# The maxima of the next chunk two slots later, and the expert weights at the end of a step

## The reference, cut to what matters

```
xn = _layernorm(x)
attention: Q, K, V = low-rank projections of layernorm(xn) + bias
  scores = where(causal, Q K^T / sqrt(8), -1e9);  ctx = softmax(scores) V
  h = xn + ctx @ out_U @ out_V + out_b
  branch 1 = h + gelu(layernorm(h) @ fc1_U @ fc1_V + fc1_b) @ fc2_U @ fc2_V + fc2_b
experts: top 2 of softmax(xn @ Wr), weights cw normalised over the two
  branch 2 = sum over e of cw[e] * ((silu(xn @ Wg[e]) * (xn @ Wu[e])) @ Wd[e])
out = x + branch 1 + branch 2
```

## Time and profile before

| | |
|---|---|
| time, median of 3 runs | 1030.21 us (1029.5 to 1030.91) |
| time of the profiled execution | 1029.5 us |
| its span | 1027.8 us |
| TensorE matmul | 965.2 us (94%) |
| TensorE weight load | 751.1 us (73%) |
| VectorE | 701.6 us (68%) |
| ScalarE | 539.0 us (52%) |
| GpSimd | 431.2 us (42%) |
| steps 0 to 15 of the attention | about 100.5 to 617 us |

### The profile page before, as it was taken

The page is one execution under the profiler, slowest core; times in us unless marked ns, Lnnn a source line. Parts: engine busy times, 40 slices in busy tenths (PEclk is TensorE's granted clock), DMA queues, the critical chain, the costliest instruction groups (busy, mean ns, idle before and its releaser), DMA issues. The chain is left out here.

```text
span 1027.8 us, 25266 instructions
## 1 busy us (share of the span) xinstructions
PE 965.2 (94%) x7701; PEld 751.1 (73%) x7701; DVE 701.6 (68%) x3192; ACT 539.0 (52%) x1256; POOL 431.2 (42%) x563
## 2 busy tenths in 40 slices
PE   4767999999999999999999988999999999999997
PEld 3535566666666666666666647999999999999986
DVE  5557688877778778777777853565565554558887
ACT  1552355555555555555555664555555555554442
POOL 9361132154544544435555422554544544540100
PEclk9585899999999999999999998999999999999999
DMA  8284454354554555353443204222222222238784
GB/s 234 72 236 136 168 178 174 106 154 135 130 142 130 141 143 136 99 135 111 140 116 117 80 28 123 64 64 66 68 69 63 66 64 62 74 111 248 208 224 134
DMA packets 133558, 127.13 MB, mean 124 GB/s; under 512 B 17274, under 2 KB 113652, under 8 KB 133428
## 3 DMA queue, kind: packets, MB, share of 16 engines
q1 hardware_dynamic: 109860, 67.83, 24.3%
q0 software_dynamic: 20592, 56.43, 17.8%
q10 hardware_dynamic: 2976, 1.26, 0.5%
HBM read 57.15 MB, written 42.60 MB: 97 GB/s over the span
## 5 line engine op out<-in xcount | busy, mean ns | idle before, releaser
L1393 DVE CUSTOM_DVE_ANT_0 att_masked_st<-att_m_ps,att_mask_st 128x128 bf16<-128x128 f32 (+1 forms) x1024 | 311.0, 353 | 106.9 <-PE att_m_ps L999 61.0
L817 ACT ACTIVATE att_probs<-att_t_ps 128x512 f32<-128x512 f32 x384 | 229.2, 598 | 211.1 <-PE att_t_ps L1023 204.6
L1641 POOL DMA_INDIRECT y_scratch<-moe_y,moe_row_now x136 | 132.2, 972 | 152.6 <-DVE moe_y L1895 109.3
L652 POOL DMA_INDIRECT slot_x<-att_xs,att_slot_now x128 | 126.8, 991 | 164.2 <-PE att_t_ps L1023 145.7
L1889 DVE TENSOR_TENSOR moe_hidden<-moe_gate,moe_up_ps 128x352 f32<-128x352 f32 x136 | 70.9, 521 | 112.8 <-ACT moe_gate L1816 111.6
L1023 PE MATMUL att_t_ps<-att_mask_ts,att_ident_b 128*128 128x256 bf16 (+1 forms) x384 | 123.7, 322 | 0.0
L1718 PE MATMUL moe_y_ps<-w_down,moe_hidden_t 128*128 (+1 forms) x816 | 113.9, 275 | 1.4 <-DVE moe_y L1895 1.2
L1816 ACT ACTIVATE moe_gate<-moe_gate_ps 128x352 f32<-128x352 f32 x136 | 63.0, 463 | 96.5 <-PE moe_up_ps L1701 96.5
L1718 PEld LDWEIGHTS moe_y_ps<-w_down,moe_hidden_t 128*128 128x128 f32 (+1 forms) x816 | 101.8, 191 | 2.7 <-issue 2.6
L1393 DVE DVE_READ_ACCUMULATOR2_ANT att_row_max<- 128x1 f32 x1024 | 84.6, 83 | 0.1
L1022 PE MATMUL att_t_ps<-att_odd_stack,att_k_stack 97*128 97x512 f32 x192 | 81.3, 424 | 3.0 <-DMA att_odd_stack<-att_neg_max 2.6
(11 more groups left out here) (264 smaller groups left out, 2067.3 us busy)
## 6 DMA issues: line engine op xcount, KB each, us to landing
att_k_stack<-att_qk_parts POOLq DMA_DIRECT2D x96, 128.0 KB, 3.4
slot_x<-att_xs POOLq DMA_DIRECT2D x17, 516.0 KB, 3.2
moe_x<-slot_x SPq DMA_DIRECT2D x34, 258.0 KB, 2.8
att_xs<-xn_scratch SPq DMA_DIRECT2D x32, 256.0 KB
mlp_rows<-y_scratch POOLq DMA_DIRECT2D x16, 512.0 KB, 5.3
even_stack<-att_qk_parts SPq DMA_DIRECT2D x192, 32.0 KB
att_odd_stack<-att_qk_parts SPq DMA_DIRECT2D x192, 32.0 KB
xn_scratch<-att_probs POOLq DMA_DIRECT2D x16, 256.0 KB, 3.0
```

What stands on the lines that cost most here:

```text
L652: pool.indirect_dma_start(env["slot_x"][:], bass.IndirectOffsetOnAxis(ap=slot_now[c.parity][:, col:col + 1], axis=0), xs[c.parity][:, t, k ...
L817: act.activation(probs[:, m % PT, :], t_ps[m % 2][:], ACT.Exp).then_inc(exp_done, 1)
L1393: last = dve.tensor_tensor_reduce(out=masked_st[m % 2][:, part], in0=m_ps[m % 2][:, part], in1=mask_st[:, SEQ - width:], scale=1.0, scalar ...
L1641: pool.indirect_dma_start(env["y_dram"][:], bass.IndirectOffsetOnAxis(ap=row_now[q.parity][:, t:t + 1], axis=0), y[c.parity][:], None).the ...
```

## The change

The first unit of the next chunk moves from slot 6 to slot 8 (MAX_FROM = 8). So EARLY is 16: chunk 0 has units 0 to 15 ahead of step 0 and 16 to 23 in slots 0 to 7, and each chunk after it the same, one step ahead. EARLY_LINKS is written with EARLY, and its range is 12 to 15 as before. The two weight loads of a step move from pairs 0 and 6 to the last two pairs, 10 and 11; their steps and order stay.

```
-            if pair in W_AT and LATE <= step < LATE + W_STEPS:
-                k = 2 * (step - LATE) + W_AT.index(pair)
+            if pair >= UNITS - 2 and LATE <= step < LATE + W_STEPS:
+                k = 2 * (step - LATE) + pair - (UNITS - 2)
                 return k if k < W_LOADS else None
             return None
 
-        K_SECOND_AT, K_FIRST_AT, BIAS_AT, W_AT = (1, 2, 3), (8, 9, 10), 7, (0, 6)
-
-        MAX_FROM = 6
+        K_SECOND_AT, K_FIRST_AT, BIAS_AT = (1, 2, 3), (8, 9, 10), 7
+
+        MAX_FROM = 8
         EARLY = 2 * UNITS - MAX_FROM
...
-                EARLY_LINKS = {m: 1 for m in range(UNITS, UNITS + 4)}
+                EARLY_LINKS = {m: 1 for m in range(UNITS, EARLY)}
```

## The result

The changed kernel took 1042.34 us in the median of four runs (1041.32 to 1045.42), the kernel before 1030.24 us beside it: a ratio of 1.012, 95% interval 1.010 to 1.014. The forecast was 1031.0 us with a range up to 1034.8, so the result lies well above the range, on the side of the rivals that made the weight loads dear.

A forecast was written before the change was run, and what follows sets the result against it. TensorE was taken to bound the steady steps, VectorE the stretch before the tile count. Start -2.4, last step +0.6, turn 0 and loads +2.6 gave +0.8 us on the 1030.21 median: 1031.0 us, range 1028.4 to 1034.8.

The forecast's parts named there:

- the rivals that made the weight loads dear: Pair 10 loads hold the copy: full price 1036.9 us, chance 0.08; prices in between, around 1034 us, 0.18.
- term 4: Steps 3 to 10: weight loads in pairs 10 and 11 delay the copy of negated maxima; +2.6 us, 0 to 7.
- What bounds the kernel: TensorE bounds steady steps, VectorE the stretch before the tile count; the maxima copy has about 0.3 us to spare.
- Term 1: Ahead of step 0's tile count: two fewer units for VectorE bring the count earlier; -2.4 us, gain 1.4 to 3.4.
- term 2: Last step: eight units where it had six, two more wide ones; +0.6 us, between 0.2 and 1.4.
- Term 3: Steady steps, turns in slots 9 and 21: now need a later VectorE take; nothing, bound 5.6 us over 28 turns.
- A large load: A 528 KB load in pair 10 of steps 3, 6 and 8: 0.7 us each, between 0 and 1.1.
- A small load: A small load in pair 10 of steps 4, 5, 7, 9 and 10: 0.15 us each, between 0 and 0.85.
- every load in pair 10 holds the copy: Rival: each load, small ones too, holds the copy its full 1.4 us in 8 steps; +6.7, 1036.9 us; chance 0.08.

The follow-up runs named there:

- run 11: The kernel before, unchanged, for a second profile of it; the profiled execution took 1034.31 us.
- run 12: The kernel before with only MAX_FROM = 8 (maxima moved, loads where they were), profiled a second time; the profiled execution took 1031.80 us.
- run 1: The kernel before with the maxima alone moved (MAX_FROM = 8), weight loads left in pairs 0 and 6; 1033.73 us, ratio 1.0008.
- run 2: The kernel before with the weight loads alone moved, to pairs 10 and 11; 1047.19 us, ratio 1.0149.
- run 3: The kernel before with one weight load of each step in pair 0, the other in pair 10; 1042.07 us, ratio 1.0106.
- run 4: The kernel before with one weight load of each step in pair 0, the other in pair 11; 1033.63 us, ratio 1.0012.
- run 7: The kernel before with one weight load of each step in pair 4, the other in pair 11; 1039.45 us, ratio 1.0065.
- run 9: The changed kernel with the loads reordered so that pair 10 holds small ones alone, pair 11 the large; 1036.80 us, ratio 1.0060.
- run 6: The kernel before with the counting matmuls of step 0 moved from slot 6 to slot 7; 1036.36 us, ratio 1.0034.
- run 8: The changed kernel with the load of pair 10 one pair earlier, in pair 9; 1042.41 us, ratio 1.0086.
- run 10: The changed kernel with the load of pair 10 two pairs earlier, in pair 8; 1036.74 us, ratio 1.0058.

## Why the prediction was wrong

The step that failed is term 4, the price of the weight loads: the sum had it at +2.6 us, and it was +10.1 in the profiled execution. What was changed and where it would hurt was foreseen, how much was not.

*What bounds the kernel*: right. Steps 11 to 14 and 1 and 2 kept their time to 0.3 us, and the short chain behind L1053 with its 0.3 us to spare was where the loss came.

*Term 1, the start, -2.4 us (1.4 to 3.4)*: the count came at 110.54 instead of 112.41, 1.9 us earlier, and 2.1 us between runs 11 and 12; at step 1 some 1.6 us are left of it in that pair, 0.4 in the mean of six against six. Right up to the count; that the gain reaches the end is not shown. What was missed is that the clock behind the count differs by 7 us of length and some 4 us of time between executions of one program. A gain of 1.0 us net (1.6 less term 2) can't be told in such runs; run 1 gives it as no difference.

*Term 2, the last step, +0.6*: right. From the first score unit to the last it took 609.39 - 585.40 = 23.99 us before and 622.78 - 598.20 = 24.58 after, 0.59 more. The other 2.4 us of the +3.0 in the last line of the table lie behind it; with the maxima moved alone the whole stretch of that line took 1032.5 - 587.9 = 444.6 us in run 1 and 1030.1 - 587.2 = 442.9 in run 12, so it varies by itself.

*Term 3, the turn, 0*: right for the turn. No idle time in front of L1053 in the steady steps, and run 1 is the same as before. That the later maxima bring longer waits for the copy, about 1 us (run 1), stands in no term; it is as much as the net gain that the terms 1 and 2 leave.

*Term 4, the loads, +2.6 (0 to 7)*: here it failed, and in the size, not the place. The mechanism (a load issued up to 1.1 us ahead of the copy holds it, and TensorE stands one for one in the first score unit of the next step) is shown by runs 2, 3, 4 and 7. Of the sum in the prediction these parts were off:

- A large load: taken as 0.7 us, "between 0 and 1.1". Measured 1.73, 1.60, 1.54, a mean of 1.62, above the bound. The bound was 1.4 us of hold less 0.3 to spare; the 1.4 came from one window that began 1.9 us after an issue, and it was taken as the length of the whole hold, with nothing added for the copy's own packets behind it. In steps 3 and 8 the copy then had 2 us without a packet, and its last two packets came up to a microsecond behind the others.
- A small load: taken as 0.15 us on the ground that "the sync queue went on moving". It did, with 30 packets of 32 in run 9. But the copy lands with its last packet. Measured 0.74, 0, 1.93, 0, 0.62, a mean of 0.66; more than the bound of 0.85 once.
- The clock: not in the term at all. Behind two of these waits the granted clock was 0.50 for 3.4 us each, and TensorE's work in steps 3 to 10 took 3.8 us longer, 3.5 of it in the two steps with that clock. In run 9, with waits of at most 1.10 us, it did not fall.

Together +10.1 us in place of 2.6; the idle time alone, +6.3, is inside the bound of 7, and with the clock it is not. The rival "every load in pair 10 holds the copy", at 1036.9 us and 0.08, was the nearest and still too cheap by the clock and by the full hold of the large ones.

The Trainium skill, "DMA: Bandwidth & Descriptors", section on queues, rings and completion order, has an engine drain a packet of many descriptors before it turns to another queue. Behind the large loads the sync queue moved 0 packets in a microsecond to 67 and 82 of POOL's. The trace agrees with the rule if the profile's packets are the page's descriptors: 0.34 MB in 82 of them is 4.1 KB each, so by estimate a load of 528 KB has about 8 for each of the 16 engines, few enough for one packet of the page. No run shows which of the two the profile counts. Behind a small load 30 of 32 moved on time and two were late, which fits the rule if it is read for each engine by itself. The prediction set it aside for the small loads on the queue's mean rate, which says nothing about the slowest engine.

*What stays open*: on which engine the last two packets stand, and why a small load holds them in some steps and not in others; when a wait of this length brings the clock down; why the copies are waited for longer with the maxima moved; and why run 6 lost 0.3%. No version here beat the kernel before by more than can be told.

## What to carry to other kernels

Before moving a bulk load of another queue, find the small copies that something on the critical path waits for, and issue the load behind them: here 0.9 us behind cost nothing that could be told, 1.1 us ahead cost 1%, 3.2 to 4.0 us ahead 0.9%, and 3.8 to 5.2 us ahead still 0.6%. Judge a delay of a small copy by when its last packet lands, not by whether its queue went on moving, and bound it by the whole load, not by a window of it. And before reading a few microseconds out of one profile, take a second one of the same program.

## What the runs showed of the hardware

- A copy of 32 packets on the sync queue did not move at all for 2 us behind a 528 KB load of POOL's queue, and the matmul that needs it came 4.0 to 4.2 us behind the issue, 2.69 before. Behind a 192 KB load (run 9, step 3) 30 packets moved on time and two did not; over all small loads of the changed kernel the matmul came 2.3 to 4.4 us behind the copy's issue.
- In a stretch where TensorE was otherwise busy throughout, its granted clock was 0.50 for 3.4 us after it had idled 1.60 and 1.93 us (341.2 and 375.3), and 1.00 again after that; after 1.73 and 1.54 us (243.22 and 409.75) it stayed. In steps 3 to 10 of the changed kernel and runs 2, 3, 7, 8 and 10 there are 19 waits of 1.40 to 2.43 us; the granted clock fell behind 10 of them and stayed at 1.00 behind 9, among these waits of 2.01 and 1.92 us. It fell behind none of the shorter waits, the longest of which is 1.25 us.
- The length of the stretch at the low clock in step 0 was 6.8 or 13.7 us in two executions of one program. With the count one slot later no idle time stood right in front of it (0.79 and 1.14 us stood 1.6 and 1.3 us ahead of it), and it was 13.6 and 17.0 us. Runs of the kernel before, 72 of them beside the experiments, lay between 1025.12 and 1038.23 us.
